# Scatters and early gathers of the sorted projection: at most two indirect transfers under way

## What is computed

```
for f in q, k, v:
    for _ in range(4):                       # a tree of 15 nodes
        score = sum(xf * node_w[cur]) + node_b[cur]
        cur = 2 * cur + 1 + (score >= 0)
    leaf = cur - 15                          # one of 16 leaves
    hidden = relu(xf @ w1[leaf] + b1[leaf])  # 256 -> 64
    out_f = hidden @ w2[leaf] + b2[leaf]     # 64 -> 256
x = x + 0.5 * softmax(q k^T / 16) v
```

## Time and profile before

| | us |
|---|---|
| median of 3 runs | 3553.56 |
| lowest and highest | 3543.06, 3554.68 |
| the profiled execution | 3545.07 |
| its span, first to last instruction | 3543.4 |
| TensorE busy in it | 2965.5 |
| VectorE busy | 2119.5 |
| GpSimd busy | 795.3 |

### The profile page before, as it was taken

How to read it: one execution, slowest core, us unless ns; L and a number is a source line. 1 busy time by engine, 2 the same in 40 slices (tenths; PEclk the granted TensorE clock), 3 DMA queues, 4 the chain that set the end, 5 groups by cost and what they waited for, 6 DMA issues and landing times. The chain is left out here.

```text
span 3543.4 us, 54686 instructions
## 1 busy us (share of the span) xinstructions
PE 2965.5 (84%) x20622; PEld 1771.0 (50%) x20622; DVE 2119.5 (60%) x3299; ACT 1785.6 (50%) x3479; POOL 795.3 (22%) x1400
## 2 busy tenths in 40 slices
PE   4158689999688999999999999999674157689999
PEld 2046578888343333333333333333341046578888
DVE  4023345544347899999999999995244023345554
ACT  3024334333121788888888888888342034333333
POOL 1721321000013122222222222211021722221000
PEclk7578789999795999999999999999897578799999
DMA  9447511010557454444444455440324347411100
GB/s 285 150 143 223 163 48 41 28 32 22 190 204 87 47 64 56 56 57 56 56 56 56 60 61 61 55 51 9 107 97 103 127 150 227 151 44 41 32 27 23
DMA packets 455582, 314.03 MB, mean 89 GB/s; under 512 B 166859, under 2 KB 430032, under 8 KB 455328
## 3 DMA queue, kind: packets, MB, share of 16 engines
q1 hardware_dynamic: 421408, 226.66, 31.8%
q0 software_dynamic: 33920, 83.93, 7.4%
HBM read 183.16 MB, written 130.97 MB: 89 GB/s over the span
## 5 line engine op out<-in xcount | busy, mean ns | idle before, releaser
L1414 DVE TENSOR_REDUCE mx_ha<-s_ps_ha 128x2 f32<-128x1024 f32 x1024 | 1242.6, 1221 | 109.7 <-PE s_ps_ha L1321 104.9
L1479 ACT ACTIVATE probs_ha<-s_ps_ha 128x512 f32<-128x512 f32 x2048 | 1109.0, 595 | 223.3 <-PE s_ps_ha L1332 90.7
L1321 PE MATMUL s_ps_ha<-ks_ha,qs_ha 48*128 48x512 f32 x2048 | 763.7, 456 | 18.7 <-DMA ks_ha<-parts_d 13.2
L1332 PE MATMUL s_ps_ha<-qs_ha,ks_ha 50*128 50x512 f32 x2048 | 753.4, 448 | 0.9 <-ACT probs_ha L1479 0.2
L1343 PE MATMUL o_ps_ha<-probs_ha,vs_ha 128*32 128x256 f32 (+1 forms) x7936 | 652.0, 401 | 21.5 <-DVE oT_ha L1441 21.5
L1321 PEld LDWEIGHTS s_ps_ha<-ks_ha,qs_ha 48*128 48x128 f32 x2048 | 315.7, 191 | 455.4 <-DVE mx_ha L1414 358.2
L413 DVE COPY y_p<-y_ps_p 128x256 f32<-128x256 f32 x282 | 119.5, 424 | 463.0 <-remote 296.7
L836 ACT ACTIVATE probsT_a<-pT_ps_a 128x512 fp32r<-128x512 f32 x256 | 146.4, 597 | 424.4 <-PE pT_ps_a L709 424.4
L1343 PEld LDWEIGHTS o_ps_ha<-probs_ha,vs_ha 128*32 128x32 f32 x7936 | 156.9, 108 | 383.1 <-issue 182.1
L1332 PEld LDWEIGHTS s_ps_ha<-qs_ha,ks_ha 50*128 50x128 f32 x2048 | 307.5, 186 | 32.7 <-ACT probs_ha L1479 32.2
L529 PE MATMUL h_ps_p<-xsT_p,wa_p 128*65 128x128 f32 x1128 | 186.9, 291 | 114.2 <-issue 92.4
(11 more groups left out here) (188 smaller groups left out, 3919.1 us busy)
## 6 DMA issues: line engine op xcount, KB each, us to landing
xs_p<-xs_d SPq DMA_DIRECT2D x66, 512.0 KB
ys_d<-y_p SPq DMA_DIRECT2D x66, 512.0 KB
qs_ha<-parts_d SPq DMA_DIRECT2D x192, 128.0 KB, 6.2
ks_ha<-parts_d SPq DMA_DIRECT2D x192, 128.0 KB, 7.0
parts_d<-parts_hp POOLq DMA_DIRECT2D x32, 512.0 KB, 3.2
xs_d<-y_p SPq DMA_DIRECT2D x15, 1024.0 KB, 10.8
leaf_w_p<-in_wa SPq DMA_DIRECT2D x6, 1040.0 KB
leaf_w_p<-in_wb SPq DMA_DIRECT2D x6, 1040.0 KB
```

The lines of the kernel that those rows point to most:

```text
L1321: nc.tensor.matmul(s1_ps[:, e % BANKS, :], qs[0:QKROWS, n % SLOTS, c, :], ks[0:QKROWS, n % SLOTS, g * 4:(g + 1) * 4, :].rearrange("p c t - ...
L1332: nc.tensor.matmul(out, ks[LOW:LOW + KR, n % SLOTS, c, :], qs[LOW:LOW + KR, n % SLOTS, g * 4:(g + 1) * 4, :].rearrange("p c t -> p (c t)") ...
L1414: nc.vector.reduce_max(mx[:, at:at + 2], s1_ps[:, e % BANKS:e % BANKS + 2, :], AX_X).then_inc(s1_free, 1)
L1479: nc.scalar.activation(probs[:, (n + c) % (LATE + 1), g * 512:(g + 1) * 512], s2_ps[:, turn % TURNS, :], ACT.Exp).then_inc(s2_free, 1)
```

## The change

Every scatter and every early gather now waits, before it is issued, until the indirect transfer two places ahead on POOL has landed. Two semaphores, `moved[0]` and `moved[1]`, take the place of `scattered` and `early_rows`; even transfers count on one and odd ones on the other, from the first scatter to the last early gather. SP's first load of each f waits for both. The order of the instructions is the same on all engines, and nothing is added but waits.

```diff
-        early_rows = ctx.enter_context(nc.semaphore(f"early_rows_{tag}"))
-        scattered = [ctx.enter_context(nc.semaphore(f"scattered{f}_{tag}")) for f in range(FF)]
+        moved = [ctx.enter_context(nc.semaphore(f"moved{u}_{tag}")) for u in range(2)]
...
             def load_rows(g):
                 if g % PER_F == 0:
-                    sp.wait_ge(scattered[ORDER[g // PER_F]], 16 * GT)
+                    for u in range(2):
+                        sp.wait_ge(moved[u], 16 * (g // PER_F + 1) * GT // 2)
...
                 for t in range(GT):
+                    if k * GT + t >= 2:
+                        pool.wait_ge(moved[t % 2], 16 * ((k * GT + t) // 2))
                     pool.indirect_dma_start(xs_d[f], bass.IndirectOffsetOnAxis(slots[:, f, t:t + 1], 0),
-                                            xn[:, t, :], None).then_inc(scattered[f], 16)
+                                            xn[:, t, :], None).then_inc(moved[t % 2], 16)
...
                 for t in range(QT):
+                    pool.wait_ge(moved[t % 2], 16 * ((FF * GT + i * QT + t) // 2))
                     dst = k_rows[:, t * D:(t + 1) * D] if f == 1 else v0[:, t, 1, :].bitcast(F32)
                     pool.indirect_dma_start(dst, None, ys_d[f],
-                                            bass.IndirectOffsetOnAxis(slots[:, f, t:t + 1], 0)).then_inc(early_rows, 16)
-            pool.wait_ge(early_rows, 16 * 2 * QT)
+                                            bass.IndirectOffsetOnAxis(slots[:, f, t:t + 1], 0)).then_inc(moved[t % 2], 16)
+            for u in range(2):
+                pool.wait_ge(moved[u], 16 * (FF * GT + 2 * QT) // 2)
```

## The result

The changed kernel took 3405.11 us (median of 4 runs, 3396.08 to 3421.39); the kernel before, measured beside it, took 3554.12 us (4 runs, 3543.06 to 3558.25). The ratio is 0.959, 95% interval 0.955 to 0.963. The forecast was 3410.

The account below looks back on a forecast made before the run. It took TensorE's pauses beside indirect transfers in `fff_project` as the bound: 216 us excess, less 28, 22 and 20 given back, gains 146; less 6 and 3 leaves 137, so 3545 becomes 3408, forecast 3410 (range 3350 to 3590; likeliest case 3365 to 3480).

Parts of the forecast that it names:

- The excess of the pauses: Three TensorE pauses in each pass of `fff_project`, beside scatters and early gathers: together 216 us over clean tiles.
- Given back: Part of the 216 us in `fff_project` not gained: 28 us for DMA, 22 for clock, 20 for gathers.
- a fuller DMA: Tiles of f = 1 and 64 scatters share the DMA engines at 0.9: 14 us more a pass, 28 in all.
- a low clock: Waits on a full DMA make gaps that lower TensorE's clock: 11 us a pass, 22 in all (0 to 90).
- The gathers' remainder: Early gathers meet the third `leaf_w` load; a third of their pauses' excess stays, 20 us in all (0 to 61).
- what is late next: Scatters of f = 2 must land near 179 us, 1.65 us each; slower, SP holds the load, delaying stores and TensorE.
- Free flow: Waits add 0.05 us a transfer (0 to 0.10) ahead of the first load: 3 us in all (0 to 6).
- Term (a), the start of pass 1: Pass 1, 83 to 99 us: scatters beside `leaf_w` loads fall behind; first load 6 us later (0 to 7.6).
- a pile: Work left by transfers delays TensorE; the burst of five at the first loads piles up some 6 us, POOL's pitch prevents draining.
- signs of being right: New profile: 45 matmuls per 10 us from 140 to 220, prompt L445, slower pitch beside tiles, `fff_project` 50 to 90 us shorter.
- signs of being wrong: L529 to L445 still 8 to 10 us, first load over 10 us later, or f = 2 scatters landing after 180 us.
- The waits feed the pause: Rival in `fff_project`: the pause follows transfer flow, so delaying POOL lengthens it; 3561 or 3588 us, chance of slower 0.30.

Follow-up runs that it names:

- before again: The kernel before, unedited, run again on another chip with its trace: 3339.09 us with its profile, 3326.74 us beside.
- the second set: Kernels before and after, unedited, on another chip, with two edited kernels: before 3339.09 with its profile and 3326.74 beside, after 3392.92 us.
- paced: The kernel before, without waits on transfers, POOL clearing an unread buffer ahead of each scatter of f = 2 and f = 0: 3365.06 and 3369.82 us.

## Why the prediction was right, point by point

**The total.** 3410 was forecast and 3405 came. The profiled execution is 140 us shorter; the sum said 137. By stretches: the start gave back 13.5 us against 7.6 in the sum, the projections gained 149.3 against 146, and the other two stretches gained 4.4 where the sum had a loss of 1.6. That the misses cancel to 3 us is luck; that the long pause and its size carry the result is not. The parts show how much of the agreement was earned.

**The excess of the pauses: right.** 216 us over clean tiles were summed, 109 and 107 a pass. The kernel before without a pause has projections of 195.2 and 194.3 us against 297.1 and 297.5: 102 and 103 us. My "clean" was too clean by 7 us in pass 1 and 4 in pass 2.

**Given back, 70 us: right in size, wrong in cause.** 35 us a pass were to go to a fuller DMA, a low clock and the gathers. The changed kernel's projection of pass 1 is 35 us above the clean one (223.0 against 297.1 - 109.2 = 187.9). But 7 of these are there without any wait, and the other 28 are TensorE waiting for rows that POOL had not scattered in time, at f = 2 and again at f = 0. The three terms as such were poor. The gathers' remainder of 10 us a pass isn't there: beside ten transfers issued from 277 to 301 us, before again does 159 matmuls in 24 us at a clock of 1.00; the 89 of the changed kernel in that stretch have the hold of f = 0 in it, which ends at 286.12. The loss of clock is there, but mostly behind the holds: 0.56 from 210 to 220 us in after. Against these stood a step that the prediction named ("what is late next") and did not price: 32 transfers must go at 1.65 us each or SP holds the load. The threshold was right, since 1.68 us costs nearly nothing and 2.10 us does. The pace was there to be estimated and I left it out: it should have been a term, (2.1 - 1.65) x 32 = 14.4 us at f = 2, where SP was held for 15.0. At f = 0 the prediction names no limit at all, and SP was held for 13.1.

**Free flow: right.** The pitch rose from 1.27 to a mean of 1.33 us (gaps of 0.31 and 0.45 in turn), 0.06 a transfer against 0.05 and inside 0 to 0.10.

**Term (a), the start of pass 1: mis-sized.** 6 us, bounds 0 to 7.6; the first load came 13.5 us later. 1.25 us of that isn't the change's (its first scatter started that much later), and 31 pitches at 0.06 are 2 us, so the leaf weights' load cost about 10 us. The step that failed is "at 99 it has issued about 8": it had issued four, and five at 102.69. I had let landings go on at the rate of a full queue; with two under way POOL stood for 5.84 and 7.08 us, each time for a transfer that landed late beside the load on q1 (q1 took 100.5% of the DMA engines from 86.2 to 93 us). With four under way POOL stood for 2.33 and 4.31 us there, and the first load was 6.6 us later than in before again, 1.0 of it by a later first scatter (84.74 against 83.78).

**Why the pause goes: not shown.** The forecast rested on a pile that starts in the burst at the first loads and that POOL's pace keeps up. Before again has the burst and the pace and no pause. So the burst is not sufficient. That two under way removes the pause where it exists is shown by the one comparison, whose changed kernel ran under the condition too; whether by the number, the pace or the missing burst is open. No later run met the condition, so none of the experiments made for that question could answer it. Nor is it shown what three or four under way would do there.

**The signs named beforehand.** Of the signs of being right, L449 came 0.64 us after L533, the pitch beside leaf tiles was above 1.5 us, and the projections were shorter by 74 and 75 us. The first, 45 matmuls or more in every 10 us from 140 to 220, held in five of eight stretches: 19 from 140 to 150, 24 from 200 to 210 and 28 from 210 to 220. Of the three signs of being wrong, two came: the first load was more than 10 us later, and the scatters of f = 2 landed after 180 us (SP's load is at 209.16) and held the stores. The number came out well with both, because a hold of 15 us is small beside a pause of 77.

**The rival on the other side came true elsewhere.** "The waits feed the pause" (3561 to 3588) didn't happen. But the prices behind it, waits that cost what they cost, are what is left when there is no pause: 54 us in the second set, of which 12.3 at the start, 27.3 and 25.1 in the projections, less 10 in the stretch between, which is its scatter. The prediction had no case for a kernel before that pauses in one comparison and not in others; all its executions shown were from the same comparison, and I took their agreement within 0.4% for a property of the kernel.

**The rule that spoke against.** The SBUF page of the Trainium skill ("SBUF — State Buffer", Who interferes with whom) says that DMA never contends with a compute engine and that PE waits on nobody. I set it aside by the rows of the first trace. The trace of before again agrees with it: scatters at a pitch of 1.27 us and a DMA share of 0.98 beside 453 matmuls in 82 us. The trace of before in the first comparison doesn't look like it, 10 us from L529 to L445; what delays it there isn't shown. What the rule got right is that the transfers alone don't do it.

## What to carry to other kernels

Executions that agree within 0.5% are one sample if they come from one place: before a kernel is tuned against a pause, run the kernel elsewhere and see whether the pause comes along. To know whether a condition was there in a given execution, look at a stage that the edit leaves alone. Before a limit is put on the transfers under way, work out the pitch that the reader allows (here 1.65 us) and read the pitch under load for each limit, for every group that is read; four under way cost nothing that could be measured here, two cost 2%. Whether four would have taken the pause away isn't shown. A filler that slows one engine can slow its neighbours: compare the mean times of their instructions before a pace is blamed. Cut the span at marks that the edit can't move, since a stretch that is all but unedited varies here by 23 us.

## What the runs showed of the hardware

The same program, with the same instructions on POOL at the same times and the same packets, had TensorE do 32 matmuls in 82 us in one execution and 453 in another; the link that was late, a TensorE start and the engine that waits for it, took 10 us in the one; the other kept TensorE at its pace. With it TensorE's granted clock went from 0.93 to 0.52 in that stretch. Some 205 of 3545 us hung on it in the projections (102 and 103), and by their times it was the same in all four executions of the first comparison. The cause isn't known.

The share that indirect transfers get of the DMA engines falls with their number under way while SP's queue moves rows. From 139 to 207 us, packets of q0 and q1 in before again and then in after:

```profile
q1 hardware_dynamic: 14729, 13.65, 69.9%
q0 software_dynamic: 2469, 6.75, 26.4%
```

```profile
q0 software_dynamic: 1537, 4.20, 16.7%
q1 hardware_dynamic: 10960, 10.88, 53.4%
```

2469 packets are 51 transfers in 68 us without a limit; 1537 are 32 with two under way, one in 2.1 us, while in free flow two under way gave one in 1.33 us. The limit that is nearly invisible on an empty DMA (1.33 against 1.27 us) costs over a third of the pace beside the rows.

A memset of 128x1024 on GpSimd every 2.10 us slowed VectorE's copies of the leaf weights beside it: in paced a copy took 548 ns in the mean and 1806 ns at most, in before again 240 and 469 ns.
